# Output rows of three attentions, made two tiles at a time beside the value projections

## What is computed

```python
qh = (q @ Wq.T + bq).reshape(B, L, H, E)
kh = (k @ Wk.T + bk).reshape(B, S, H, E)
vh = (v @ Wv.T + bv).reshape(B, S, H, E)
scores = jnp.einsum('blhe,bshe->bhls', qh, kh)
scores = scores * tau[:, None, None, :] + delta[:, None, None, :]
a = jax.nn.softmax(scale * scores, axis=-1)
out = jnp.einsum('bhls,bshd->blhd', a, vh).reshape(B, L, D)
return out @ Wo.T + bo
...
x = x + _L1_xcond_ref(_layernorm(x, axis=-1), ctx_1024, ctx_1024, ...)
```

## Time and profile before

| | |
|---|---|
| median of three runs | 3013.32 us |
| profiled execution, its own time | 3013.75 us |
| its span | 3011.9 us |
| PE busy | 2834.1 us (94%) |
| DVE busy | 2101.6 us (70%) |
| ACT busy | 1144.9 us (38%) |
| POOL busy | 985.1 us (33%) |
| first scores of the three attentions | 27.4, 813.9, 2582.1 us |
| last scores of the three attentions | 263.9, 1051.9, 2817.3 us |

### The profile page before, as it was taken

The page is one execution under the profiler, slowest core; times in us unless marked ns, Lnnn a source line. Parts: engine busy times, 40 slices in busy tenths (PEclk is TensorE's granted clock), DMA queues, the critical chain, the costliest instruction groups (busy, mean ns, idle before and its releaser), DMA issues. The chain is left out here.

```text
span 3011.9 us, 60068 instructions
## 1 busy us (share of the span) xinstructions
PE 2834.1 (94%) x23998; PEld 2127.4 (71%) x23998; DVE 2101.6 (70%) x6115; ACT 1144.9 (38%) x1759; POOL 985.1 (33%) x1024
## 2 busy tenths in 40 slices
PE   8998999999899989897999999999999997999798
PEld 5665776566566656576888888888888886666565
DVE  6776356110287789665999989999999988577734
ACT  5654211222366679554222222222222220555432
POOL 1332000233233322000444444444444444233355
PEclk9999999999999999998999999999999997999999
DMA  4101210234401000402120000000000001110067
GB/s 145 44 30 52 67 44 22 72 102 126 126 30 44 16 12 1 149 20 95 45 90 5 5 5 5 5 5 5 7 5 5 5 5 32 58 44 30 14 213 250
DMA packets 112675, 152.90 MB, mean 51 GB/s; under 512 B 14608, under 2 KB 92688, under 8 KB 112016
## 3 DMA queue, kind: packets, MB, share of 16 engines
q1 hardware_dynamic: 100608, 126.89, 12.8%
q0 software_dynamic: 10752, 21.11, 2.8%
q10 hardware_dynamic: 1040, 1.05, 0.1%
HBM read 102.76 MB, written 46.27 MB: 49 GB/s over the span
## 5 line engine op out<-in xcount | busy, mean ns | idle before, releaser
L2218 POOL TENSOR_TENSOR pk_hisig<-pk_hihot,pk_sigs 128x512 f16<-128x512 f16 x512 | 520.3, 1043 | 663.4 <-DVE pk_hihot L2494 661.9
L2316 PE MATMUL pk_ps<-X,dw_downT 128*128 128x256 f32 x2048 | 480.8, 386 | 0.0
L2362 PE MATMUL pk_ps<-ew_up,pk_act_h 128*128 128x256 f32 x2048 | 459.1, 383 | 1.7 <-DVE pk_act_h L2482 1.7
L2362 PEld LDWEIGHTS pk_ps<-ew_up,pk_act_h 128*128 128x128 f32 x2048 | 388.8, 191 | 57.0 <-issue 2.0
L2316 PEld LDWEIGHTS pk_ps<-X,dw_downT 128*128 128x128 f32 x2048 | 381.2, 191 | 60.2 <-issue 14.8
L2226 ACT ACTIVATE pk_act_h<-pk_ps 128x512 f32<-128x512 f32 x256 | 153.0, 598 | 546.7 <-PE pk_ps L2316 546.7
L2495 DVE TENSOR_TENSOR pk_lohot<-pk_iota_h,pk_ps 128x1024 f16<-128x1024 f16 x256 | 311.3, 1216 | 0.0
L678 DVE TENSOR_REDUCE a_mx<-a_ps_s 128x8 f32<-128x1024 f32 x192 | 226.3, 1221 | 78.9 <-PE a_ps_s L517 70.3
L2482 DVE TENSOR_TENSOR pk_act_h<-pk_act_h,pk_ps 128x512 f32<-128x512 f32 x256 | 172.0, 682 | 61.0 <-PE pk_ps L2346 61.0
L342 ACT ACTIVATE a_pT<-a_ps_s 128x2048 f32<-128x2048 f32 x96 | 180.2, 1877 | 58.1 <-PE a_ps_s L534 58.1
L444 POOL TENSOR_TENSOR X<-a_y,a_tmp 128x256 f32<-128x256 f32 x96 | 69.9, 728 | 379.2 <-ACT a_y L349 377.8
(11 more groups left out here) (420 smaller groups left out, 5210.1 us busy)
## 6 DMA issues: line engine op xcount, KB each, us to landing
ro_w<-in_L_W SPq DMA_DIRECT2D x16, 1024.0 KB, 7.4
sent<-pk_zero SPq DMA_DIRECT2D x3, 3072.0 KB, 11.1
mo_xb<-sent SPq DMA_DIRECT2D x36, 256.0 KB, 4.4
made<-mo_yb SPq DMA_DIRECT2D x36, 256.0 KB, 3.8
i_ctx_t<-in_ctxT SPq DMA_DIRECT2D x16, 512.0 KB, 3.8
i_side<-in_side SPq DMA_DIRECT2D x16, 512.0 KB, 4.7
row_dram<-sh_row SPq DMA_DIRECT2D x8, 512.0 KB, 3.0
sum_dram<-sh_new SPq DMA_DIRECT2D x8, 512.0 KB, 2.9
```

Source lines behind the costliest of these rows:

```text
L2218: ins = pool.tensor_tensor(hisig[:, buf, n, :, :, :], hi, sig2.broadcast_to([P, TP, 2, ECH]), ALU.mult)
L2316: ins = pe.matmul(hid.bank(f"h{c}")[:, j * 2 * P:(j + 1) * 2 * P], downT[:, k, e * P:(e + 1) * P], XT[:, p, k, :], start=(k == 0), stop=(k ...
L2362: ins = pe.matmul(tail.bank("y")[:, 0:D], act_h[:, p % 2, c, s * P:(s + 1) * P], up[:, c, :], start=(c == 0), stop=(c == ECH - 1))
```

## The change

`output_rows` no longer stands in every tile. It makes two tiles at once, m standing for tiles 2m and 2m + 1, and only at places 2 and 3 of a group, where the first filler is one of values. The bank `ps_y` is used in full, one emptying on ACT takes both tiles, and `oT` and `y` get four places. On POOL the two tiles' additions follow in the next tile, on DVE their statistics in the tile after that. So the statistics of two rows stand at places 0 and 1, and none at places 2 and 3. At the end of an attention the last pair is made in one piece, four rows are left to POOL (three before) and six to the statistics on DVE (three before).

```diff
-        oT = sb("oT", [P, 2, KC, P])
-        y = sb("y", [P, 2, D])
+        oT = sb("oT", [P, 4, KC, P])
+        y = sb("y", [P, 4, D])
...
+        def pair_at(t):
+            g, u = t // G, t % G
+            return {2: 2 * g - 1, 3: 2 * g}.get(u, -1)
+
+        def pair_rows(t):
+            m = pair_at(t)
+            return (2 * m, 2 * m + 1) if m >= 0 else ()
...
-                act.activation(y[:, t % 2, :], ps_y[:, 0:D], ACT.Copy).then_inc(y_taken, 1)
+                act.activation(y[:, m % 2 * 2:m % 2 * 2 + 2, :].rearrange("p a n -> p (a n)"), ps_y[:, :],
+                               ACT.Copy).then_inc(y_taken, 1)
...
-                if t >= 3:
-                    outputs(t - 3)
+                if t and pair_at(t - 1) >= 0:
+                    outputs(pair_at(t - 1))
...
-                if t >= 3:
-                    rows(t - 3)
+                if t:
+                    for r in pair_rows(t - 1):
+                        rows(r)
...
-            for t in range(TILES - 3, TILES):
+            for t in range(TILES - 4, TILES):
                 rows(t)
...
-                for k in range(KC):
-                    ins = pe.matmul(ps_y[:, 0:D], oT[:, t % 2, k, :], wo[:, k, :], start=(k == 0), stop=(k == KC - 1))
+                for n in range(2):
+                    for k in range(KC):
+                        ins = pe.matmul(ps_y[:, n * D:(n + 1) * D], oT[:, (2 * m + n) % 4, k, :], wo[:, k, :],
+                                        start=(k == 0), stop=(k == KC - 1))
...
-                if t >= 2:
-                    output_rows(t - 2)
+                if pair_at(t) >= 0:
+                    output_rows(pair_at(t))
...
-            for t in (TILES - 2, TILES - 1):
-                output_rows(t)
+            output_rows(TILES // 2 - 1)
...
-                if t >= 3:
-                    row_stats(t - 3)
+                if t >= 2:
+                    for r in pair_rows(t - 2):
+                        row_stats(r)
...
-            for t in range(TILES - 3, TILES):
+            for t in range(TILES - 6, TILES):
                 row_stats(t)
```

More of the change, by code:

```diff
@@ L343, in exps, with outputs @@
                                ACT.Exp).then_inc(p_taken, 1)
-            def outputs(t):
-                act.wait_ge(y_full, t + 1)
-                if t >= 2:
-                    act.wait_ge(x_ready, t - 1)
-                act.activation(y[:, t % 2, :], ps_y[:, 0:D], ACT.Copy).then_inc(y_taken, 1)
+            def outputs(m):
+                act.wait_ge(y_full, m + 1)
+                if m >= 2:
+                    act.wait_ge(x_ready, 2 * (m - 1))
+                act.activation(y[:, m % 2 * 2:m % 2 * 2 + 2, :].rearrange("p a n -> p (a n)"), ps_y[:, :],
+                               ACT.Copy).then_inc(y_taken, 1)
             def first_filler(g, u):
@@ L421, in _ @@
                 tile(t // G, t % G)
-            for t in range(TILES - 3, TILES):
-                outputs(t)
+            for m in (TILES // 2 - 2, TILES // 2 - 1):
+                outputs(m)
             ready_root(act, keep)
@@ L442, in rows @@
                 pool.wait_ge(tmp_ready, t + 1)
-                pool.wait_ge(y_taken, t + 1)
-                pool.tensor_tensor(x, y[:, n, :].rearrange("p (a n) -> p a n", a=1),
+                pool.wait_ge(y_taken, t // 2 + 1)
+                pool.tensor_tensor(x, y[:, t % 4, :].rearrange("p (a n) -> p a n", a=1),
                                    tmp[:, n:n + 1, :], ALU.add).then_inc(x_ready, 1)
@@ L563, in values_over_sums, with output_rows @@
                 ins.then_inc(o_full, 1)
[L565 to L568, removed]
-                for k in range(KC):
-                    ins = pe.matmul(ps_y[:, 0:D], oT[:, t % 2, k, :], wo[:, k, :], start=(k == 0), stop=(k == KC - 1))
+            def output_rows(m):
+                pe.wait_ge(turned_back, 2 * m + 2)
+                if m:
+                    pe.wait_ge(y_taken, m)
+                for n in range(2):
+                    for k in range(KC):
+                        ins = pe.matmul(ps_y[:, n * D:(n + 1) * D], oT[:, (2 * m + n) % 4, k, :], wo[:, k, :],
+                                        start=(k == 0), stop=(k == KC - 1))
                 ins.then_inc(y_full, 1)
@@ L702, in divided @@
                                   ALU.mult).then_inc(den_ready, 1)
-                if t >= 2:
-                    dve.wait_ge(y_full, t - 1)
+                if t >= 4:
+                    dve.wait_ge(y_full, t // 2 - 1)
                 dve.wait_ge(den_ready, 2 * t + 2)
-                dve.transpose(oT[:, t % 2, :, :].rearrange("p k n -> p (k n)"), rows_o[:, :]).then_inc(turned_back, 1)
+                dve.transpose(oT[:, t % 4, :, :].rearrange("p k n -> p (k n)"), rows_o[:, :]).then_inc(turned_back, 1)
             def row_stats(t):
```

## The result

The changed kernel took **3038.98 us** (median of 4 runs, 3035.17 to 3040.99); the kernel before, beside it, 3012.54 (4 runs, 3010.07 to 3016.87). The ratio is 1.0086 [1.0072, 1.0101]: slower, as forecast, but by 26 us where 11 were forecast, and outside the range. The profiled execution took 3039.50 us with a span of 3037.7, which is 25.8 more than the span before.

The account below looks back on a forecast made before the run. It took PE to bound places 0 and 1, the chain over the exponentials places 2 and 3. Per attention -10.4 + 5.3 + 5.4 + 3.0 = +3.3, three times +9.9, with tiles 6 +11.1: 3024.4 us, range 3014 to 3031.

Parts of the forecast that it names:

- the steady state: Scores to scores in a group: 7.55 us at places 0 and 1, 8.5 to 8.6 at place 2, 7.7 at place 3.
- the 0.90: Place 2: two rows' statistics on DVE delay the maxima, so turned scores start 0.90 us late; +5.4 us per attention.
- Tiles 28 and 29 have no fillers and are bound by the exponentials: Tiles 28 and 29 of an attention: bound by the exponentials, so left out of the 12 tiles that gain 0.87 us.
- The end of an attention, +3.0: Last pair starts only when tile 31 is turned: 0.87 + 0.21 + 1.46 + 0.44 = +3.0 us per attention.
- The hold of the division: End of an attention: an addition on POOL holds tile 31's division on DVE, +0.44 us.
- Rival 2: The clock falls more: one more 1.2 GHz stretch per attention, half lost, 5.0 us in all, 3029.4 us; chance 0.08.
- the forecast wait: Tile 6, first two attentions: late maxima from both rows' and arrived rows' statistics, turned scores at 83.89, tile 9.52 us.
- the forecast gain: Places 0 and 1: output rows leave, 0.87 us saved in each of 12 tiles, -10.4 us per attention.
- Rival 1: DVE is not late at the end of place 1, or too little to matter: 3007.0 us; chance 0.12.
- rival 3: The ends of attentions are hidden by something the next layer waits for anyway: 3015.4 us; chance 0.06.

Follow-up runs that it names:

- stats_apart: The changed kernel with the second pair's statistics moved from place 1 to places 2 and 3, one row each: 3017.73 us.
- busy_last: The changed kernel with two unread products of 128 x 256 put into tiles 28 and 29 on PE: 3029.57 us.
- before_starved: The kernel before the change, with the output products made in tiles 28 and 29 cut from 256 columns to 8: 3020.97 us.
- last_pair_split: The changed kernel with rows 30 and 31 made, emptied and added one by one at the end: 3027.92 us.
- the tail runs: 18 or 6 unread products behind the last output row: on stats_apart, last_pair_split and busy_last combined 3018.07 and 3003.49 us; 18 on the kernel before, 3030.63 us.

## Why the prediction was wrong

The direction and the steady state were right, to one or two hundredths of a microsecond per tile, and by the mechanism that was forecast: stats_apart takes the 0.90 away. What failed is that every stretch was summed at full clock. Of the 14.9 us between forecast and profile the low clock takes some 12: 3.7 in tile 29, 3.4 between the last scores and the last values, 3.4 in the last pair and 1.7 in a tile 6. Three statements failed.

- **"Tiles 28 and 29 have no fillers and are bound by the exponentials", costed at nothing.** Their length is bound so, but their output rows were work that held the clock. Without them PE is busy 3.72 of 6.82 us in tile 28 in place of 4.59, and the clock was granted at 0.50 from its end on (first attention). Tile 29 cost +3.7, and busy_last and before_starved show the cause from both sides.
- **The end of an attention, +3.0**, summed at full clock. Its steps are there, but the last pair waits until both tiles are turned, and behind that wait most of it runs at 1.2 GHz: 3.29, 2.86 and 3.29 us in the three ends, where the forecast counted 1.13 + 0.87 = 2.00. That is 3.4 of the 6.4 that the ends cost beyond the forecast. Another 3.4 come ahead of it: in the first two ends the low clock of tile 29 lasts past the last scores, and the last values (line 570) start 1.63 and 1.72 later after them than in the kernel before, in the third end 0.03. The hold of the division was sized too large: from the division to its transposition the three ends take 0.35, 0 and 0.57 longer than before, where the sum has 0.44 each. Made singly (last_pair_split), the rows run at full clock and the ends cost 5.2 in place of 15.4.
- **Rival 2 ("the clock falls more", 0.08).** It was the right kind with the wrong place and size. It looked only behind an attention, after PE's idle stretch, and the tail runs found no cost of the clock there; the fall in the last pair, behind PE's wait, comes nearest to it. It was never asked which stretches lose work and keep their length.

Smaller: tile 6 of the second attention lost its clock behind the forecast wait (+1.7 against the first), and tile 8 of the first two attentions, bound by ACT's change of table, gave none of the forecast gain (2 x 0.87 = 1.7). The remaining +1.1 is spread over other stages; no run was made on it.

Rival 1 fell by the rows of DVE, rival 3 by the ends. The Trainium skill, page "SBUF — State Buffer", section "Who interferes with whom", says that a VectorE instruction with two SBUF inputs contends with a GpSimd instruction that reads SBUF, and that whoever issues first has the shared ports for the whole instruction. The trace agrees: where the addition starts first (2853.25 against 2853.26), the division takes 1.00 us beside its 0.72, and where both start at 1081.88, the division takes 0.42 and the addition 1.01. So the hold that the prediction called sure hung on a lead that was not there in two of three ends.

What stays open is why the same thinned stretch kept its clock in 3 of 15 attentions.

## What to carry to other kernels

Where a tile's length is set by another engine, PE's work in it is not free to take away: ask of each stretch that loses work and keeps its length what the granted clock will be, and cost the next stretch on the path at half clock. Work that is moved together brings its followers together, here two rows' statistics and three POOL instructions; spread these before judging the move, since the pairs were worth 10 us once the statistics were spread, the last two rows single and the clock of tile 29 held (6 us without the unread products). At the end of a stage, work should stay in single steps that overlap.

## What the runs showed that I had not expected

The clock fell without a long idle time of PE: in tile 28 of the first attention after, no wait of PE is longer than 1.63 us, and PE was busy 3.72 of the 6.82 us before the tile that ran at 1.2 GHz. The Trainium skill, page "TensorE: Matmul & The Clock Gate", section "What's actually happening", calls the throttled state the default, which activity releases; the two runs with added and removed work agree with that (tile 29 of the first attention at 1.00 and 6.83 us with work put back, at 0.50 and 8.67 with work taken away).

A kernel with 24 more instructions on PE than the change ran 9 us faster, and one with fewer columns than the kernel before 8 us slower.
